# Moving one of two subtractions per chunk from VectorE to GpSimd in the projection of a latent-attention kernel

## What is computed

```python
c_q = x @ W_dq
Q = (c_q @ W_uq).reshape(Bx, Sx, N_HEADS, D_K)
c_kv = x @ W_dkv
K = (c_kv @ W_uk).reshape(Bx, Sx, N_HEADS, D_K)
V = (c_kv @ W_uv).reshape(Bx, Sx, N_HEADS, D_K)
scores = jnp.einsum('bqhd,bkhd->bhqk', Q, K) / math.sqrt(D_K)
...
x = x + _layernorm(_L0_attn_ref(_layernorm(x, axis=-1), L0_attn_W_dq, L0_attn_W_uq, L0_attn_W_dkv, L0_attn_W_uk, L0_attn_W_uv, L0_attn_W_o), axis=-1)
```

## Time and profile before

| what | value |
|---|---|
| median of 3 runs | 1332.39 us (1330.47 to 1337.42) |
| profiled execution | 1332.19 us |
| its span, first to last instruction | 1330.4 us |
| mean granted TensorE clock | 0.985 |
| busy: PE, DVE, ACT, POOL | 92%, 84%, 69%, 57% of the span |
| end of the first block (last L274 on VectorE) | 46.4 us |
| first matmul of the second block | 46.73 us |

### The profile page before, as it was taken

One profiled execution on the slowest core, in us unless ns is written; L12 is line 12 of the kernel. 1 busy time (PEld: TensorE's weight loads), 2 busy tenths in 40 slices (PEclk: granted clock), 3 DMA queues, 4 the chain that ended last, 5 costly groups with the idle time before them and its releaser, 6 DMA issues. The chain is left out here.

```text
span 1330.4 us, 30437 instructions
## 1 busy us (share of the span) xinstructions
PE 1223.1 (92%) x10593; PEld 714.4 (54%) x10593; DVE 1112.2 (84%) x2911; ACT 921.2 (69%) x2463; POOL 757.4 (57%) x770
## 2 busy tenths in 40 slices
PE   6889999999999999888999999799899999997895
PEld 3634344444444433455666666566466666665653
DVE  6898989998899897689899998665798999997675
ACT  6356777877777787677888888423788888885344
POOL 5212223312332232498999999431899999996244
PEclk9989999999999999999999999899999999998998
DMA  5311331122111101012111111100112111110001
GB/s 133 117 52 64 92 90 54 51 62 65 48 45 39 42 5 59 17 33 47 34 26 33 34 33 26 41 1 1 26 32 55 34 27 32 34 33 17 1 17 48
DMA packets 38830, 56.47 MB, mean 42 GB/s; under 512 B 7170, under 2 KB 23948, under 8 KB 38668
## 3 DMA queue, kind: packets, MB, share of 16 engines
q1 hardware_dynamic: 37864, 54.19, 15.3%
q10 hardware_dynamic: 816, 0.34, 0.2%
HBM read 27.78 MB, written 8.39 MB: 27 GB/s over the span
## 5 line engine op out<-in xcount | busy, mean ns | idle before, releaser
L1164 ACT ACTIVATE a_prob<-a_psE 128x512 f32<-128x512 f32 (+1 forms) x608 | 303.3, 593 | 133.1 <-PE a_psE L769 131.5
L1566 DVE CUSTOM_DVE_ANT_0 a_psM<-a_psM,mask_q 128x384 f32<-128x384 f32 (+3 forms) x512 | 234.5, 521 | 33.7 <-PE a_psM L753 33.2
L1399 POOL TENSOR_SCALAR_AFFINE_SELECT a_prob<-a_prob 128x512 f32<-128x512 f32 x128 | 80.8, 638 | 311.4 <-ACT a_prob L1164 307.7
L1458 POOL TENSOR_TENSOR w_rn<-w_ssm,mhalf 128x16 f32<-128x16 f32 x64 | 220.4, 3444 | 49.6 <-DVE w_ssm L1658 34.2
L769 PE MATMUL a_psE<-a_qs,a_ks 84*128 84x512 bf16 (+3 forms) x768 | 235.8, 330 | 9.7 <-ACT a_prob L1164 6.9
L753 PE MATMUL a_psM<-a_ks,a_qs 72*128 72x512 bf16 (+3 forms) x768 | 236.1, 330 | 4.2 <-DVE a_nm L1566 2.1
L1274 ACT ACTIVATE w_prob<-w_psS,w_bias 128x128 f32<-128x128 f32 x512 | 179.8, 377 | 20.3 <-DVE w_bias L1684 20.3
L1443 POOL TENSOR_TENSOR w_t<-w_raw,w_sin 128x256 f32<-128x256 f32 x252 | 176.4, 731 | 0.0
L1568 DVE TENSOR_REDUCE a_nm<-a_psM 128x1 f32<-128x512 f32 x256 | 158.6, 681 | 12.8 <-PE a_psM L753 11.5
L1448 POOL TENSOR_TENSOR w_rot<-w_t,w_t 128x1024 f32<-128x1024 f32 x63 | 148.6, 2358 | 8.7 <-issue 0.4
L769 PEld LDWEIGHTS a_psE<-a_qs,a_ks 84*128 84x128 bf16 x768 | 73.6, 97 | 144.2 <-ACT a_prob L1164 77.7
(11 more groups left out here) (193 smaller groups left out, 2451.2 us busy)
## 6 DMA issues: line engine op xcount, KB each, us to landing
a_qs<-q_parts SPq DMA_DIRECT2D x32, 288.0 KB
a_ks<-k_parts SPq DMA_DIRECT2D x32, 288.0 KB
q_parts<-p_parts SPq DMA_DIRECT2D x24, 128.0 KB
k_parts<-p_parts SPq DMA_DIRECT2D x24, 128.0 KB
w_vb__699<-w_v__683 SPq DMA_DIRECT2D x16, 128.0 KB, 2.2
w_vb__700<-w_v__683 SPq DMA_DIRECT2D x16, 128.0 KB, 2.3
w_vb__700<-w_v__684 SPq DMA_DIRECT2D x16, 128.0 KB, 2.2
w_vb__701<-w_v__684 SPq DMA_DIRECT2D x16, 128.0 KB, 2.4
```

What stands on the lines that cost most here:

```text
L1164: act.activation(prob[G % NPROB][:, j - share + 1:j + 1, 0:w], psE[:, r % NRING, 0:share * w].rearrange("p (j n) -> p j n", j=share), ACT. ...
L1458: pool.tensor_tensor(rn[:, T % 2, 0:n], ssm[:, T % 2, 0:n], sb["mhalf"][:, 0:n], ALU.pow).then_inc(rn_done, 1)
L1566: d = dve.tensor_tensor_reduce(scores, scores, sb["mask_q"][:, 512 - n:512], -1.0, -3.0 * NEG, ALU.add, ALU.min, low)
```

## The change

Of the two subtractions L274 of each chunk, that of q stays on VectorE as `low_q`; that of k becomes a step `low_k` on GpSimd, with lag 3, behind `middle`. It waits for GpSimd's own second cast. SyncE waits for both results before it sends chunk 0 or 1. VectorE's `remainder` of chunk c gets one more wait, that `low_k` of chunk c-2 is done, since that reads the same half of `p_rem`. The data and the arithmetic are the same.

```diff
         @block.sync
...
             for c in range(2):
-                sp.wait_ge(parts_done, 2 * c + 2)
+                sp.wait_ge(low_q_done, c + 1)
+                sp.wait_ge(low_k_done, c + 1)
                 send_parts(sp, io, sb, c)
...
+            def low_k(c, par):
+
+                place = c % PARTS
+                pool.wait_ge(mid_done, 2 * c + 2)
+                pool.tensor_tensor(parts[place][:, 1, 2, :], rem[:, par, 1, :], parts[place][:, 1, 1, :], ALU.subtract).then_inc(low_k_done, 1)
+
             pool.wait_ge(ones_set, 3)
-            pipelined(pool, NCH, 2, [(0, powers), (3, middle)])
+            pipelined(pool, NCH, 2, [(0, powers), (3, middle), (3, low_k)])
...
             def remainder(c, par):
 
+                at_least(dve, low_k_done, 0, c, -1)
                 for w in range(2):
...
-            def low(c, par, w):
+            def low_q(c, par):
 
                 place = c % PARTS
-                dve.wait_ge(mid_done, 2 * c + w + 1)
-                dve.tensor_tensor(parts[place][:, w, 2, :], rem[:, par, w, :], parts[place][:, w, 1, :], ALU.subtract).then_inc(parts_done, 1)
+                dve.wait_ge(mid_done, 2 * c + 1)
+                dve.tensor_tensor(parts[place][:, 0, 2, :], rem[:, par, 0, :], parts[place][:, 0, 1, :], ALU.subtract).then_inc(low_q_done, 1)
...
-            pipelined(dve, NCH, 2, [(1, shifts), (0, mean_and_weights), (3, remainder), (3, low_q), (3, low_k)])
+            pipelined(dve, NCH, 2, [(1, shifts), (0, mean_and_weights), (3, remainder), (3, low_q)])
```

## The result

| | median | lowest to highest | runs |
|---|---|---|---|
| kernel before | 1332.41 us | 1330.22 to 1339.17 | 22 |
| changed kernel | 1335.37 us | 1333.91 to 1342.95 | 22 |

The ratio is 1.0022, with a 95% interval of 1.0012 to 1.0032: the change costs 1.6 to 4.3 us, which is clear of no change and far under 0.5% (6.7 us). The profiled execution has a span of 1333.1 us against 1330.4. The forecast was 1334.8 and no change beyond 0.5%.

The account below looks back on a forecast made before the run. First block's barrier waits for VectorE's chunk 7 subtraction, though TensorE is busiest overall (92%). Hand-over 2.3 + tail 0.3 = +2.6 us on span 1330.4 gives span 1333.0, time 1334.8; range 1330.0 to 1337.2.

Parts of the forecast that it names:

- The turns: First block: a VectorE instruction with two SBUF inputs and a GpSimd instruction that reads SBUF take turns.
- The rival in which VectorE keeps its turn: Chunks 0 to 4: shift takes the ports before GpSimd; five slots win 0.60 each, block -1.4, time 1330.8; chance 0.22.
- a dear GpSimd with bf16: Rival, all eight `low_k`: beyond 1.77 us each, over 0.5% slower; 1343.6 at 2.36; chance 0.04.
- The hand-over: Chunks 0 to 4: shift waits for GpSimd's `low_k`, loop 0.46 longer per slot, 2.3 us in all; chance 0.60.
- the price of `low_k`: GpSimd's 128x512 subtraction of k, taken as 1.26 us from L1496, the row with the same operation and size.
- its reading starts before the recorded end of the VectorE instruction: At `low_k` behind `low_q`: waiting GpSimd starts reading 0.15 before VectorE's recorded end (0.73 - 0.58).
- A reading of the prediction: First block's loop: VectorE's subtraction of k separates the end of the first (31.77) from the shift by 0.60.
- Five of them: Chunks 0 to 4, chunk 0 included: all five slots have the same order, 5 x 0.46 = 2.3 us.
- The tail: Chunks 5 to 7: no shift follows, GpSimd's chain counts; the block ends 0.3 us later, bounds 0 and 0.6.
- Moved waits: SyncE's first send 0.5 us later, last load ending at 45.0, covered by GpSimd; VectorE's new wait costs nothing.
- TensorE's wait for the small DMA: Wait of 1.08 us that may shrink; up to 0.5 may come back, none counted.
- The second block should only move: Second block, behind the barrier: only shifted in time; a change of more than 1 us there would show the forecast wrong.

Follow-up runs that it names:

- k3b_after_warm: Changed kernel with matmuls of 512, 512 and 256 columns in TensorE's idle time at the first block's end; median 1334.85 against 1332.88 us, ratio 1.0009.
- k3_after_warm: Changed kernel with five matmuls of 128x512 float32 behind TensorE's last one in the first block; median 1337.62 us, ratio 1.0026 to the kernel before.
- k10_after_again: Changed kernel unaltered, profiled once more; median 1335.15 us against 1334.25 for the kernel before, ratio 1.0013.
- k5_before_warm: Kernel before with two matmuls of 128x512 float32 behind TensorE's last one in the first block; median 1334.10 us, ratio 1.0000.
- k2_delay: Kernel before with a memset of 128x1600 behind VectorE's last subtraction of the first block; median 1334.76 against 1333.94 us, ratio 1.0011.
- k4_early_shift: Changed kernel with each chunk's shift in its own slot, between VectorE's remainders and `low_q`; median 1332.49 us against 1333.94 for the kernel before, ratio 0.9986.

## Why the prediction was right, and where it was not

*The turns.* The mechanism and its place were as forecast: subtraction of q 1.06, shift held to 1.11 and ending 0.02 behind GpSimd's, GpSimd served between VectorE's two instructions. The rival in which VectorE keeps its turn is refuted, as is a dear GpSimd with bf16 (1.15 where nothing holds it).

*The hand-over was mis-sized:* 0.36, not 0.46. The step that failed is the price of `low_k`, taken as 1.26 from L1496 in the earlier trace rows. Its own time is 1.15 where nothing holds it (46.91, above), and the difference is the 0.10. The other part of that step held: its reading starts before the recorded end of the VectorE instruction, by 1.15 - 1.02 = 0.13 where 0.15 was taken. The figure of the Trainium skill ("SBUF — State Buffer", section "A bandwidth-pool intuition that's wrong (but worth ruling out)"), some 115 ns behind that end, is given there for DMA descriptors that GpSimd writes, and the trace does not show it for a subtraction. The rule of its section "Who interferes with whom", that the later one to issue of a VectorE instruction with two SBUF inputs and a GpSimd one that reads SBUF waits until the other is over, agrees with the subtractions and casts of the first block. No such wait is seen beside GpSimd's power instruction in the second block of the kernel before, with a VectorE shift whose two inputs are in SBUF:

```profile
582.96 2.90 POOL L1458 TENSOR_TENSOR w_rn<-w_ssm,mhalf 128x16 f32<-128x16 f32 x1
```

```profile
584.24 0.16 DVE L1596 SCALAR_TENSOR_TENSOR m_shift<-m_mv,w_rn 128x8 f32<-128x8 f32 x1
```

That shift was issued in the middle of the power instruction and took 0.16. So how long a GpSimd instruction holds VectorE differs between its operations, and only subtractions and casts are priced here.

*A reading of the prediction* was loose: between 31.77 and the shift at 32.30 lie 0.53, not 0.60. The 0.60 is the shift moved to 31.70, with the 0.07 by which VectorE's records overlap, and the sum used it in that way.

*Five of them was too many.* In chunk 0 the remainder of k came late (0.81 of waiting for ScalarE), VectorE's subtraction of q went ahead of the cast of k, and the shift was held 0.57 only. In the profiled pair slot 3 even got shorter (4.64 against 4.91). This was in part luck of the pair. In k3b_after_warm the same code had the full hand-over in chunk 0 (shift 1.11, slot 5.27), in k3_after_warm and k10_after_again the slot took 5.26 and 6.44, with waits of 0.80 and 2.00 for the load of `x`, while the kernel before took 5.14 in k5_before_warm and 5.15 in k2_delay. In the profiled pair the block ended 1.65 later; between k3 and k3b (48.66, 48.55) and k5 and k2 (46.38, 46.23) it is 2.2 to 2.4. Slots 4 to 7 gave 4 x 0.36 = 1.44, by experiment 1.46. Forecast for all five: 2.3.

*The tail* cost 0.56 instead of 0.3, still in the bounds of 0 to 0.6. The step that failed: I let the last cast of k go first, but VectorE's subtraction of q took its turn before it, and that cast took 1.08 (45.75 to 46.83) instead of 0.61. In k4_early_shift the last casts did go first, and from the first cast to the end of the last subtraction it took 2.76 (41.82 to 44.58) instead of 3.04 (45.02 to 48.06): 0.28, the size of the miss.

*Moved waits.* SyncE's first send came at 18.46 instead of 17.70, 0.76 and not 0.5 later; its last load ended at 45.29, under GpSimd's 48.06, so it cost nothing, as said. TensorE's wait for the small DMA of the earlier trace rows, which might have shrunk, was 1.16 instead of 1.08.

*"The second block should only move"* was wrong, by 1.1 us in the profiled pair, which is over the 1 us that I had named as a sign of error. The block alone gave 1.69 in that pair; the forecast of 2.6 for the whole met 2.7 because a term that I had not seen (1.1, TensorE at 1.2 GHz behind the barrier) made up for what I had counted too high in the first block. The mechanism in the first block was right; that the number came so close was luck.

*What stays open.* The code's own cost is about 2.0 us from slot 4 on. How much of the 0 to 1.5 us at the barrier belongs to the change can't be told: from first matmul to first maximum it was 3.37 and 3.38 in the two profiles of the changed kernel, but 2.08 and 2.71 in two others with the same idle time of 3.19 to 3.20, and 2.26, 1.90 and 3.38 in three kernels with a shorter one. With the idle time filled it was 1.90 in four executions of four, unfilled in one of ten; that a longer idle time makes it worse was not shown. Nor is it known why executions of the unchanged second block drift apart by 1 to 2 us at other places.

## What to carry to other kernels

Before work goes from VectorE to GpSimd, look at what VectorE issues next: an instruction with two tensor inputs in SBUF, however small, stood here until a GpSimd subtraction or cast issued before it was over, while one with a single such input, the other in PSUM or a scalar per partition, didn't. GpSimd's power instruction did not hold one. Here the offload cost 0.36 us per slot with a shift of 128x4 behind it, and gained 0.6 per slot (4.82 to 4.23) when the shift went to a place where VectorE waited anyway. When a sum of small terms meets the measurement, compare each term with its row, since here errors cancelled, and take more than one profile, since the unchanged part of this program moved by 1 to 2 us between executions.

## What the runs showed of the hardware

The mixed subtraction on GpSimd (float32 minus bf16, bf16 out) is faster than the float32 one of the same shape, 1.15 against 1.26 us. GpSimd casts are held too: 1.08 and 1.01 instead of 0.61 when VectorE's two-input instruction came first. Four VectorE instructions with a scalar per partition from SBUF were not held (0.57 beside a running GpSimd subtraction, 0.58 with GpSimd idle), so such a scalar didn't count as a second input. And TensorE's granted clock at one place differed between executions of the same code: the same instructions took 1.90 to 3.38 us to the first result, with 1.2 GHz in none, part or all of the stretch, while four executions in which TensorE had idled for no more than 1.05 us all had 2.4 GHz and 1.90.
